# Moving the attention statistics two blocks ahead, the row normalisation one step ahead, and one product from VectorE to GpSimd

## What is computed

```python
mod = (_silu(c) @ wmod).reshape(16, 6, 1, -1)
sa, ca, ga, sb, cb, gb = mod[:, 0], ..., mod[:, 5]      # ga, gb clamped away from 0
h = _layernorm(x) * (1 + ca) + sa                       # first modulation
q, k, v = phi(h @ W_q), phi(h @ W_k), h @ W_v           # phi = elu + 1
o = causal_sum(q k^T) v / max(sum(q * cumsum(k)), 1e-6)
x = x + ga * (o @ W_o)
h = _layernorm(x) * (1 + cb) + sb                       # second modulation
normed = _layernorm(h, rn_g, rn_b)
top_w, top_idx = top_k(normed @ router_w.T + router_b, 2)
for e in range(8):
    y = gelu(_layernorm(h, ln_g[e], ln_b[e]) @ w1[e] + b1[e]) @ w2[e] + b2[e]
    out = out + combine[..., e] * y
x = x + gb * out
```

## Time and profile before

| | us |
|---|---|
| median of 3 runs | 1125.11 |
| lowest and highest | 1123.71, 1125.61 |
| profiled execution, whole | 1125.48 |
| its span, first to last instruction | 1123.6 |
| first stage, up to the last list position | 0 to 370 |
| first expert matmul | 394.3 |

### The profile page before, as it was taken

One profiled execution on the slowest core, in us unless ns is written; L12 is line 12 of the kernel. 1 busy time (PEld: TensorE's weight loads), 2 busy tenths in 40 slices (PEclk: granted clock), 3 DMA queues, 4 the chain that ended last, 5 costly groups with the idle time before them and its releaser, 6 DMA issues.

```text
span 1123.6 us, 31567 instructions
## 1 busy us (share of the span) xinstructions
PE 988.9 (88%) x8116; PEld 806.3 (72%) x8117; DVE 889.1 (79%) x3010; ACT 542.9 (48%) x1123; POOL 573.6 (51%) x478
## 2 busy tenths in 40 slices
PE   5777879887945099999999999999999999999997
PEld 1334545554534088888888888888888888888875
DVE  5578999999985567777877877877877877877776
ACT  1668787878843134434444443444443443444443
POOL 2121666666667536655455445445445445545543
PEclk8798888888965599999999999999999999999999
DMA  4465777876869466665565555566555556566453
GB/s 134 133 227 194 237 230 260 291 271 212 315 233 401 122 185 132 137 123 92 96 118 98 106 112 104 98 109 99 94 108 103 90 108 108 87 120 122 88 100 49
DMA packets 162626, 169.80 MB, mean 151 GB/s; under 512 B 89340, under 2 KB 136968, under 8 KB 158472
## 3 DMA queue, kind: packets, MB, share of 16 engines
q1 hardware_dynamic: 129736, 114.24, 36.5%
q0 software_dynamic: 32832, 54.88, 25.3%
HBM read 94.67 MB, written 62.78 MB: 140 GB/s over the span
## 4 chain that ended last, share of the span: by engine, by line
PE 66%; issue 8%; DVE 8%; POOL 6%; ACT 2%; DMA 1%; POOLq 0%; DVEq 0%; SPq 0%; ACTq 0%
PE banks L1440 32%; PE banks L1452 31%; POOL lists L551 5%; PE banks L1334 2%; DVE st L771 2%; POOL rs L544 2%; DVE store L968 1%; PE banks L1322 1%; ACT rowbuf L628 1%; DVE mv L779 1%; ACT store L712 1%; DVE rowbuf L908 1%; DMA out<-rowbuf,ydst 0%; DVE store L926 0%; DVE ix L1001 0%
## 5 line engine op out<-in xcount | busy, mean ns | idle before, releaser
L1440 PE MATMUL banks<-nhl,store 128*128 128x256 bf16 (+1 forms) x3408 | 450.5, 268 | 28.0 <-DMA nhl<-xhl 24.8
L740 ACT ACTIVATE gf<-banks,b1t 128x256 f32<-128x256 f32 (+1 forms) x568 | 263.0, 463 | 429.1 <-PE banks L1440 411.7
L1452 PE MATMUL banks<-store 128*128 x3240 | 448.0, 273 | 0.5
L1440 PEld LDWEIGHTS banks<-nhl,store 128*128 x3408 | 324.1, 98 | 71.0 <-issue 30.1
L587 POOL DMA_INDIRECT out<-rowbuf,ydst x135 | 223.7, 1657 | 294.1 <-DVE rowbuf L1222 222.0
L1452 PEld LDWEIGHTS banks<-store 128*128 128x128 bf16 x3240 | 310.5, 98 | 41.9 <-issue 1.8
L1231 DVE CAST store<-gf 128x256 bf16<-128x256 f32 (+1 forms) x568 | 180.5, 318 | 130.7 <-ACT gf L740 99.3
L1233 DVE TENSOR_TENSOR store<-gf,store 128x256 bf16<-128x256 f32 (+1 forms) x568 | 234.7, 413 | 19.5
L551 POOL DMA_INDIRECT lists<-store,slot x128 | 141.0, 1102 | 96.3 <-issue 49.0
L578 POOL DMA_INDIRECT store<-y_rows,ygb x135 | 135.2, 1001 | 63.3 <-issue 51.8
L544 POOL TENSOR_TENSOR rs<-ve,mhalf 128x12 f32<-128x12 f32 (+2 forms) x20 | 39.0, 1950 | 84.6 <-DVE ve L786 84.5
(11 more groups left out here) (225 smaller groups left out, 970.0 us busy)
## 6 DMA issues: line engine op xcount, KB each, us to landing
rowbuf<-lists SPq DMA_DIRECT2D x64, 264.0 KB
store<-in_L_ffn_w SPq DMA_DIRECT2D x16, 1024.0 KB, 6.0
wsplit<-store SPq DMA_DIRECT2D x16, 1024.0 KB, 5.7
store<-wsplit SPq DMA_DIRECT2D x16, 1024.0 KB, 11.1
b2t<-in_L_ffn_b SPq DMA_DIRECT2D x71, 128.0 KB
store<-in_L_attn_x SPq DMA_DIRECT2D x16, 512.0 KB, 9.6
out<-store SPq DMA_DIRECT2D x16, 512.0 KB, 9.9
csB<-mod_rows SPq DMA_DIRECT2D x16, 256.0 KB, 4.0
```

The costliest lines, as they stand in the source:

```text
L740: a.activation(gf[:, c % 2, 0:halves(j) * P], MM[c % 2][:, 0:halves(j) * P], ACT.Gelu, bias=b1t[:, r, c:c + 1]).then_inc(gf_s, 1)
L1440: last = t.matmul(MM[c % 2][:, 0:halves(j) * P], w, nhl[:, r, m, 0:halves(j) * P], start=n == 0, stop=n == 5)
L1452: last = t.matmul(ACC[r][h][:, 0:D], g[:, c, h * P:(h + 1) * P], w, start=c == 0 and n == 0, stop=c == NI - 1 and n == 2)
```

## The change

`h2m`, the product of the second modulation, leaves DVE and becomes a POOL operation between `wog` and the first scatter. DVE keeps the sum. The statistics of a block's attention rows are now made two steps ahead (in step i for block i+2, with those of block 1 added to the setup), and ACT writes `xc` for block i+1 near the end of step i, not for block i at the start of step i; PE's transposes stay where they were. The counts of `rs`, `nm` and `ve` grow by one. SP loads one block further ahead: in step 0 blocks 2 and 3, in step i block i+3. The router's bias moves on DVE from the end of the setup to the end of step 0, and PE waits for it in step 1.

```diff
             def load_x(i, half, r):
...
+                for b in range(2 if i == 0 else i + 3, min(i + 4, NB)):
+                    sp.wait_ge(got_x[b % 2], 16 * (b // 2))
+                    sp.dma_start(resid[:, b * NC:(b + 1) * NC, :], x_v[b]).then_inc(got_x[b % 2], 16)
...
+            inverse_root(-1, 1)
             inverse_root(0, 0)
...
+                if norm:
+                    b, q = i - 3, 1 - r
+                    pool.wait_ge(got_cs[q], 16 * (half if q == 0 else half - 1))
+                    pool.wait_ge(xn2_s, b + 1)
+                    wait_past(pool, nrm_s, b - 1)
+                    g.tensor_tensor(h2[q], xn2, csB[:, q, D:2 * D].unsqueeze(1).to_broadcast([P, NC, D]), ALU.mult).then_inc(h2m_s, 1)
...
+            def centred(b, r):
+
+                act.wait_ge(got_x[b % 2], 16 * (b // 2) + 16)
+                wait_past(act, xT_s, b)
+                normalise(lambda c: xc[:, c, :], rows(b), r, 0, xc_s)
+
+            act.wait_ge(nm_s, 1)
+            centred(0, 1)
...
-                if project or norm or route:
-                    act.wait_ge(nm_s, i + 1)
-                if project:
-                    act.wait_ge(got_x[r], 16 * half + 16)
-                    wait_past(act, xT_s, i)
-                    normalise(lambda c: xc[:, c, :], rows(i), r, 0, xc_s)
...
+                if 0 < i < NB - 1:
+                    centred(i + 1, r)
...
-                if project and not (isinstance(i, int) and i == NB - 1):
...
+                if i + 2 < NB:
+                    dve.wait_ge(got_x[r], 16 * half + 32)
                     hold(dve, "dve")
-                    stats(rows(i + 1), 0)
+                    stats(rows(i + 2), 0)
                 if norm:
                     b, q = i - 3, 1 - r
                     dve.wait_ge(got_cs[q], 16 * (half if q == 0 else half - 1))
-                    dve.wait_ge(xn2_s, b + 1)
-                    wait_past(dve, nrm_s, b - 1)
+                    dve.wait_ge(h2m_s, b + 1)
                     hold(dve, "dve")
-                    v.tensor_tensor(h2[q], xn2, csB[:, q, D:2 * D].unsqueeze(1).to_broadcast([P, NC, D]), ALU.mult).then_inc(h2m_s, 1)
+                    v.tensor_tensor(h2[q], h2[q], csB[:, q, 0:D].unsqueeze(1).to_broadcast([P, NC, D]), ALU.add).then_inc(h2_s, 1)
```

## The result

The changed kernel takes 1157.70 us in the median (1155.34 to 1158.71, 4 runs); the kernel before took 1125.14 us beside it. The ratio is 1.0289, 95% interval 1.0269 to 1.0308: 2.9% slower. The prediction was 1140.3 us with a range up to 1147. The sign was right and the loss was about twice as large as forecast.

The account below looks back on a forecast made before the run. DVE was taken to set the pace in steps 5 to 14, POOL in the last steps. 4.1 - 2.9 + 9.1 + 4.9 = +15.2 us gave 1140.3 us, 1.4% slower; 80% range 1122 to 1147 us.

Parts of the forecast that it names:

- Part 4: Steps 5 to 14: the product on POOL delays DVE's choice and the power still comes late; +9.1 us.
- `ohs` is held until the product's inputs are read, to 8.07: After odd steps: `oh` gets in first, `ohs` is held 2.0 us, so `slot` comes 1.25 us later.
- +0.56 us: After even steps: the product holds `pick` on DVE, whose end moves from 8.37 to 8.93.
- The first rival: No mutual hold-up of weight: `ohs` and `pick` slip past the product, power before the running sum; 1121.6 us, 14%.
- The product's price: POOL's product of 1024 elements a partition, scaled from `wog`: 2.4 us, bounds 1.2 and 3.0.
- `nm` waits for the power: Steps 5 to 14: the power meets DVE's running sum and is held, losing the 1.2 us DVE saves.
- 9.7 us from `slot` to `nm`: Middle steps: `nm` at 9.7 us after `slot`; before it was 9.5, after even steps 9.8.
- Part 1: The start: step 0's statistics wait for block 2 behind two weight loads; +4.1 us, bounds 0 to +5.
- the forecast of +1.2: Start to step 4: +4.1 us at the start, -2.9 us in steps 3 and 4.
- Part 5: Steps 15 to 18: +4.9 us, of it +0.4, +1.0, +0.35 and +3.1 by step.
- the extra hold of 0.7 us: Step 18: the sum released by POOL's product holds the next scatter 0.7 us more, within the step's +3.1.
- a dearer product: Rival: POOL's product takes 3.0 us and holds DVE 0.6 us longer in eleven steps; 1147 us, 13%.

## Why the prediction was wrong

**Part 4 failed, in one term: the length of the hold.** The mechanism was named: POOL's product and small DVE operations hold each other. The step "`ohs` is held until the product's inputs are read, to 8.07" assumed that DVE's operations go on while `wog` runs, that `oh` gets in, and that a hold begins with the product. After even steps it assumed that DVE gets its turn between `wog` and the product and reaches `pick` before it is held again (+0.56 us). Neither happened in steps 6 to 14. POOL's two operations follow each other without a gap, and one DVE operation lasts until the end of the second: a hold of 3.0 us for `dl`, 3.25 for `oh`. The row that should have warned was the earlier trace rows: `ohs` ended as `wog` did. The right question was what POOL starts at that moment. From `nm` to `slot` the forecast was 11.07 us after odd and 9.66 after even steps, measured 11.92 and 11.81. That is +0.85 and +2.15, over ten steps +15 where the total missed by 14.

**The order was never safe.** In the profile after, `wog` starts 0.36 us after `oh` in one step and 0.09 us after `dl` in the next. The first rival had the hold vanish if the operations slide past each other. The version that waits for the choice shows that this was worth 22.9 us, but it took an added wait. The changed kernel met the collision in nine of ten middle steps; only in step 15 did it go about as the prediction had it.

**What held.** The product's price, 2.4 us forecast and 2.35 measured: scaling the smaller row by its elements was right. That `nm` waits for the power (1.56 us measured), that the power takes over 3 us where it meets the sum (3.05), and 9.7 us from `slot` to `nm` (9.66, in step 9 9.94) are as forecast; the version with three scatters ahead confirms the cause. `phi` of step 0 at 37.15 us, measured 37.69, with the wait for the input in front:

```profile
35.52 1.41 DVE L783 BATCH_NORM_STATS2 st<-store 128x6 f32<-128x256 f32 x4 [10.28 <-DMA store<-in_L_attn_x]
...
37.69 0.68 DVE L940 SCALAR_TENSOR_TENSOR store<-banks,ex 128x512 f32<-128x512 f32 x1
```

**Part 1 was too large.** The forecast had +4.1 us at the start, but step 1's mask came at 46.77 us instead of 44.41, +2.4. PE's transposes and scores lie between. PE's granted clock was higher there, 0.73 from `phi` to the mask against 0.57 before, and the transposes took 1.10 us against 1.97; no run tests why:

```profile
42.61 1.10 PE L1337 MATMUL banks<-ident,rowbuf 128*128 128x128 f32 x8
```

By step 4 the difference to the forecast of +1.2 was down to 0.5 us, which is within what the start varies by (102.86 to 104.56 us for the same `nm`, above).

**Part 5: the sum was short by 2.4 us, for the same reason.** In step 16 `dl` takes 3.15 us, in step 17 `oh` takes 2.81, where the forecast had +1.0 and +0.35. In both DVE then waits 4.16 us for the power, which stands behind four scatters that start only when `slot` is there. So every delay of `slot` reaches `nm`. Step 17:

```profile
360.48 2.81 DVE L1022 TENSOR_TENSOR oh<-experts,ix 128x64 f32<-128x64 f32 x1 [0.18 <-DVE ix L1017]
...
373.91 0.21 DVE L813 SCALAR_TENSOR_TENSOR nm<-mv,rs 128x8 f32<-128x8 f32 x1 [4.16 <-POOL rs L540]
```

Step 18 was 2.1 us, not 3.1: the product took its 2.36 us between two scatters, but the extra hold of 0.7 us didn't come.

**The range.** Its upper end came from a dearer product (3.0 us), not from a longer hold, though only the hold was unknown. A hold over `wog` and product together, 0.74 and the 2.4 estimated, was a bound that the rows gave; it is what came, and steps 5 to 14 cost 14 us more than forecast.

## What to carry to other kernels

Before work moves to POOL, list which small DVE operations will run beside it, and price each at up to the full length of everything that POOL then runs without a gap. An engine that looks 40% free can still be unusable, if its work reads SBUF beside the small operations of the bound engine. Here these were operations with two SBUF inputs and one `TENSOR_SCALAR` with a single input. Where both must work at once, put POOL's reading beside DVE operations that the trace shows unharmed (here the statistics), and let what is waited for start before DVE's long operation and not after it. To tell such a collision from a dependency, let the suspected engine do the same work on constants that nobody needs.

## What the runs showed of the hardware

- A DVE operation of 4 columns, 0.15 us alone, took 3.15 us beside two POOL products, one of 64 columns 3.48; the ends followed POOL's by 0.02 to 0.08 us. In step 9 `oh` (64 columns, 0.23 us alone) has a record that begins 0.36 us before that of `wog`. Whether POOL's record begins late or DVE is held before POOL starts was not settled.
- A `TENSOR_SCALAR` with one input is held too. In the version with the input first and three scatters ahead, DVE and POOL:

```profile
180.31 2.68 DVE L1044 TENSOR_SCALAR d<-dex 128x4 f32<-128x4 f32 x1
```
```profile
180.60 2.35 POOL L562 TENSOR_TENSOR rowbuf<-rowbuf,csB 128x1024 f32<-128x1024 f32 x1
```

  The statistics (1.41 us for four, no single one over 0.43) were never longer beside POOL's product.
- Between the power and the running sum the start decides. The power, started 0.6 us before DVE's running sum, took 2.30 us and the sum its 1.22; started up to 0.3 us after the sum's start, it took 3.0 to 3.3. It is no general rule here: `oh` in step 9 starts ahead of `wog` and is held all the same.
- Beside POOL's fills, DVE's cast and copies had records up to 2.3 us long, while the instructions behind them started. The middle steps were 0.4 us longer and not 2.
- PE's granted clock differed between versions in step 17: 0.50 (1.2 GHz) in the version with only the product moved back, 0.69 in the one with three scatters and the input first as well, where the step took 15.6 us instead of 19.0. It was 0.50, and the step 19.1 us, in the two versions with POOL's product, three scatters and the input first too, so a part of the differences between whole times may be this and not POOL's work. In all four the clock had been 0.60 to 0.69 in the step before. What tips it wasn't tested.
